# Gated recurrence: VectorE in place of GpSimd multiplies the matrix for the inverse by the step sizes, just ahead of turning it

## The reference, cut to what matters

```
def step(carry, inp):
    S, R = carry
    q_t, k_t, v_t, a_t, aR_t, b_t, g_t = inp
    kn = k_t / jnp.maximum(jnp.linalg.norm(k_t, axis=-1, keepdims=True), 1e-12)
    pred = jnp.einsum('bhji,bhj->bhi', S, kn)
    r = jnp.clip(v_t - pred, -CLIP, CLIP)
    S = a_t[..., None] * S
    kp = jnp.einsum('bhd,bhde->bhe', kn, S)
    S = S + b_t[..., None, None] * kn[..., None] * (v_t - kp)[..., None, :]
    o = jnp.einsum('bhji,bhj->bhi', S, q_t)
    R = aR_t[..., None] * R
    kpR = jnp.einsum('bhd,bhde->bhe', kn, R)
    R = R + g_t[..., None, None] * kn[..., None] * (r - kpR)[..., None, :]
    o = o + jnp.einsum('bhji,bhj->bhi', R, q_t)
    return ((S, R), o)
```

## Time and profile before

| | us |
|---|---|
| median of 3 runs | 2985.55 (2983.88 to 2993.01) |
| the profiled execution, its own time | 2989.19 |
| its span in the trace | 2987.4 |
| this sublayer's steady part in the trace (13 turns, 1052 to 1839) | 787 |

### The profile page before, as it was taken

The page is one execution under the profiler, slowest core; times in us unless marked ns, Lnnn a source line. Parts: engine busy times, 40 slices in busy tenths (PEclk is TensorE's granted clock), DMA queues, the critical chain, the costliest instruction groups (busy, mean ns, idle before and its releaser), DMA issues. The chain is left out here.

```text
span 2987.4 us, 115613 instructions
## 1 busy us (share of the span) xinstructions
PE 2398.5 (80%) x49947; PEld 1861.7 (62%) x49947; DVE 1954.5 (65%) x4625; ACT 1363.1 (46%) x3250; POOL 1002.2 (34%) x1250
## 2 busy tenths in 40 slices
PE   8987478999976578888778887669998997797754
PEld 6754465555555577777777776548776654575633
DVE  3448335777756787888777888157777666564752
ACT  5443133444443344454444542447776553563420
POOL 0000324556650345434543355311111440360004
PEclk9979677999997799999999999969999998897876
DMA  3200331111110000000000000012221003242014
GB/s 99 66 1 29 114 116 53 47 47 46 47 58 3 3 4 4 4 4 4 4 4 4 4 4 4 3 27 61 63 62 58 4 3 108 64 110 66 5 43 122
DMA packets 80270, 117.47 MB, mean 39 GB/s; under 512 B 11490, under 2 KB 66034, under 8 KB 79234
## 3 DMA queue, kind: packets, MB, share of 16 engines
q1 hardware_dynamic: 71250, 100.31, 10.9%
q0 software_dynamic: 8576, 10.53, 1.7%
HBM read 98.16 MB, written 16.51 MB: 38 GB/s over the span
## 5 line engine op out<-in xcount | busy, mean ns | idle before, releaser
L2469 POOL TENSOR_SCALAR l1xs_p<-l1xs_p,l1xs_col 128x257 f32<-128x257 f32 x256 | 234.3, 936 | 204.4 <-DVE l1xs_col L2425 204.4
L3173 PE MATMUL psum<-l1d_rw,l1d_cols 64*32 64x48 f32 x16384 | 188.1, 211 | 106.1 <-issue 76.1
L3173 PEld LDWEIGHTS psum<-l1d_rw,l1d_cols 64*32 64x32 f32 x16384 | 164.4, 108 | 128.5 <-issue 118.1
L2390 ACT ACTIVATE l1xs_p<-psum,l1xs_col 128x257 f32<-128x257 f32 x256 | 119.7, 473 | 209.6 <-DVE l1xs_col L2420 203.5
L3429 DVE TENSOR_TENSOR l1d_rw<-l1d_rw,l1d_tots 128x1536 f32<-128x1536 f32 (+1 forms) x96 | 141.4, 1473 | 64.9 <-PE psum L3173 64.3
L2945 POOL TENSOR_TENSOR l1d_kc<-l1d_ms,l1d_beta 128x512 f32<-128x512 f32 x16 | 17.5, 1093 | 494.9 <-DVE l1d_ms L3484 477.9
L2432 DVE STREAM_TRANSPOSE l1xs_pt<-l1xs_p 128x288 f32<-128x288 f32 x256 | 122.4, 478 | 79.1 <-POOL l1xs_p L2469 79.0
L3112 PE MATMUL psum<-XN,l1d_wp 128*128 128x128 f32 x1024 | 142.6, 296 | 7.6 <-issue 6.7
L3112 PEld LDWEIGHTS psum<-XN,l1d_wp 128*128 128x128 f32 x1024 | 130.6, 206 | 21.0 <-issue 17.8
L2354 PE MATMUL psum<-l1xs_pt,l1xs_vals 32*128 32x512 f32 x1152 | 136.6, 604 | 0.0
L2342 PE MATMUL psum<-l1xs_keys,l1xs_qx 128*32 128x257 f32 x2048 | 132.7, 392 | 3.7 <-DVE l1xs_qx L2414 1.9
(11 more groups left out here) (563 smaller groups left out, 6852.7 us busy)
## 6 DMA issues: line engine op xcount, KB each, us to landing
l2f_w<-in_l2f_w SPq DMA_DIRECT2D x16, 768.0 KB
l1xs_vals<-in_ctx_strips SPq DMA_DIRECT2D x16, 576.0 KB
l0f_w<-in_l0f_w SPq DMA_DIRECT2D x15, 579.0 KB
l0x_ctxT<-in_ctxT SPq DMA_DIRECT2D x16, 516.0 KB, 3.7
l1xs_keys<-in_ctxT SPq DMA_DIRECT2D x16, 516.0 KB
l2x_ctxK<-in_ctxT SPq DMA_DIRECT2D x64, 129.0 KB, 2.1
l2x_ctxV<-in_ctxT SPq DMA_DIRECT2D x64, 129.0 KB, 2.1
l3f_w<-in_l3f_w SPq DMA_DIRECT2D x15, 193.5 KB
```

Source lines behind the costliest of these rows:

```text
L2390: nc.scalar.activation(p[:, t % 4, :S2], score_ps(t)[:, :S2], ACT.Exp, bias=col[:, 0, t % 4:t % 4 + 1], accum_out=col[:, 1, t % 4:t % 4 + ...
L2469: nc.gpsimd.tensor_scalar(p[:, t % 4, :S2], p[:, t % 4, :S2], col[:, 2, t % 4:t % 4 + 1], None, ALU.mult).then_inc(s["norm"], 1)
L3173: mm = nc.tensor.matmul(k.ps[bank0 + pr + e // per * 2][b * T:b * T + T, e % per * w:(e % per + 1) * w], columns[rr, at:at + T], moving[rr ...
```

## The change

The two multiplications of `gather` leave POOL's list and go into DVE's, directly ahead of the transposes of `turn`. The wait for `mS` of the next tile at level 1 is dropped; the other waits stay. Tiles, shapes and arithmetic stay the same.

```diff
-            def gather(i):
-
-                pool.wait_ge(s["mS"], i * LEVELS + LEVELS)
-                pool.wait_ge(s["mR"], i * LEVELS + LEVELS)
-                pool.wait_ge(s["beta"], i + 1)
-                if i + 1 < NT:
-                    pool.wait_ge(s["mS"], (i + 1) * LEVELS + 2)
-                if i > 0:
-                    pool.wait_ge(s["wideX"], i * 2)
-                at = kc[:].rearrange("p (t c) -> p c t", t=T)
-                minus = beta[:, i % 3, 1].unsqueeze(2).to_broadcast([128, 2 * H, T])
-                tt(at[:, :H, :], ms[:, i % 2, :, 0, :], minus[:, :H], ALU.mult)
-                tt(at[:, H:, :], mr[:, i % 2, :, 1, :], minus[:, H:], ALU.mult).then_inc(s["kc"], 1)
-
...
             for i in range(NT):
-                gather(i)
                 pool.wait_ge(s["turn"], 2 * i + 2)
                 merge(i, 2)
...
+            def gather(i):
+
+                dve.wait_ge(s["mS"], i * LEVELS + LEVELS)
+                dve.wait_ge(s["mR"], i * LEVELS + LEVELS)
+                dve.wait_ge(s["beta"], i + 1)
+                if i > 0:
+                    dve.wait_ge(s["wideX"], i * 2)
+                at = kc[:].rearrange("p (t c) -> p c t", t=T)
+                minus = beta[:, i % 3, 1].unsqueeze(2).to_broadcast([128, 2 * H, T])
+                tt(at[:, :H, :], ms[:, i % 2, :, 0, :], minus[:, :H], ALU.mult)
+                tt(at[:, H:, :], mr[:, i % 2, :, 1, :], minus[:, H:], ALU.mult).then_inc(s["kc"], 1)
+
...
                 if i == NT:
+                    gather(i - 1)
                     turn(i - 1)
...
                 if mid and now:
+                    gather(i - 1)
                     turn(i - 1)
```

## The result

| | before | changed |
|---|---|---|
| median of 20 runs each, us | 2981.32 (2969.47 to 2993.01) | 2994.48 (2982.60 to 3000.67) |
| ratio, 95% interval | | 1.0039 (1.0027 to 1.0050) |
| profiled execution, us | 2989.19 | 2994.31 |
| its span in the trace, us | 2987.4 | 2992.4 |

The account below looks back on a forecast made before the run. A ring through DVE, POOL and PE bounds each tile; the later turn passes 14 us, PE's issue gaps return half, leaving 7 us: 2985.6 + 7 = 2992.5, rounded to 2992 us (+0.2%), range 2980 to 3005.

Parts of the forecast that it names:

- What bounds the kernel: Steady tile, 60.5 us: a ring through DVE, POOL and PE, where a late turn is late again at the turn back.
- The price of the pair: Two added DVE multiplications ahead of each turn: 1.15 us each, 2.2 us together, for the 128-byte write step.
- Rival B: The pair costs a plain 1.3 us; +2.5 us, 2988 us; chance 0.22.
- The relief: DVE at L3431 and L3429 no longer meets POOL's multiplication: 0.97 us gained in 5 of thirteen tiles.
- What passes of the delay: Turn's delay passes whole in six steady tiles, 9.2 us, and 4.7 us in eight others: together 14 us.
- The covers: DVE's waits for the broadcast at L3382 hide delay in eight steady tiles, 1.3 us a tile, unevenly spread.
- I take half, between all and nothing, because the rows give no finer measure: 14 / 2 = 7 us: PE's issue gaps shrink when PE waits and give back half of the 14 us delay, leaving 7 us.
- rival A with its covers: Issue gaps give nothing back, L3382 waits still hide part of the delay: 14 us, 2999.5 us; rival A's chance 0.28.
- the prediction's own sign of it: Rival A shows if PE's wait L3161 on L3373 grows from 6.1 us and its issue gaps stay.
- The last tile: DVE's gather meets the same wait for ACT's widening; 2.08 us of POOL become 2.2 us of DVE: nothing.

Follow-up runs that it names:

- the pair behind the turn: Kernel before, POOL's gather kept, plus the same two products written by DVE into an unread spare tile directly behind the turn: 1.0065, +19.4 us.
- the second trace: Another profile of the unedited changed kernel, taken with the experiments; thirteen periods from turn 1 to turn 14 take 796.9 us.
- the pair ahead of the turn: Kernel before, POOL's gather kept, plus the same two products written by DVE into an unread spare tile ahead of the turn: 1.0073, +21.7 us.
- the kernel before with two buffers: Kernel before with a second `kc` buffer, POOL keeping the gather: 0.9971, -8.7 us.
- the one with two buffers: Changed kernel with a second `kc` buffer, so the gather needs the widening of two tiles ago: 0.9998 of before.
- the pair in the wait: Kernel before, POOL's gather kept, plus two idle DVE products into a spare tile at the iteration's start, before the wait for `fill_0`: 0.9988, -3.6 us.
- POOL's gather beside the copies: Kernel before with two `kc` buffers, POOL's gather released by the next tile's `row0` instead of `mS` at level 1: 0.9990 of before.
- The pair twice: Changed kernel plus two idle DVE products into a spare tile between gather and turn in 15 tiles: 1.0105 of before, 19.7 us above changed.

## Why the prediction was right in kind and short in size

**What bounds the kernel: right.** That the place of DVE's work decides is shown by runs: one pair costs 21.7 us ahead of the turn, nothing in the wait for `fill_0`, and moving the gather from the one place to the other won 10 us back. That it is POOL's stretch which hands the delay on is read from the traces: the turn back waits for POOL in 13 of 13 tiles of the changed kernel. No run separates this from a simpler rival, by which it costs the same in any place of DVE's list that is not a wait; the pair behind the turn cost 19.4 us, and there it also made POOL's inverse longer. From turn to turn back no steady tile of any kernel took less than 23.5 us.

**The price of the pair: right.** 1.15 us each and 2.2 us together were forecast, 1.11, 1.05 and about 2.07 us measured. The reason is shown too: the step in what is written, alone, makes 0.70 us into 1.08 (mean of the two). The Trainium skill, page "SBUF — State Buffer", section "Door 1: The DMA port swizzle", says that consecutive accesses to one 16-byte line run at full bandwidth and each crossing to a new line pays; by that rule the trace agrees, for a write as well, at a factor of 1.5. Rival B, 1.3 us for the pair, falls.

**The relief: the mechanism was right, its size in the time is open.** L3431 on 448 numbers came down to 623 ns as forecast (630). I put the relief at 0.97 us in 5 tiles, 4.9 us. In the groups it is (781 - 623) x 26 = 4.1 us at that line and (1415 - 1228) x 26 = 4.9 us at its neighbour, of which I had counted 0.6 us; the second trace has the same means, 621 and 1229 ns. In the time two measurements disagree. It is 10.7 us, with some 8 us to either side, between the pair ahead of the turn and the changed kernel. But moving POOL's gather ahead of L3429 took away the same collision at the same place and came out 5.7 us slower, again with some 8 us to either side, as other instructions stretched and DVE's waits grew. My 4.9 us lies between the two.

**What passes of the delay: 14 us raw was near.** The covers were read at `keys` (L3382) alone. The trace after shows a second one that I missed, the 9.2 us for ACT ahead of the norms, which is gone; but the norms take 9.5 us longer in exchange (1730 for 999 ns, thirteen times), so little of it was a cover. In the second trace 5.9 us of that wait are left, and the norms take 4.6 us longer; in the kernel before with two buffers it is 5.4 us, so much of the difference is scatter. Both engines' lists agree with a partial cover: DVE's waits other than the turn back fell from 125.2 to 91.4 us (108.5 in the second trace), while PE's wait for the norms rose by 10.5 us (5.0).

**The step that failed is "I take half, between all and nothing, because the rows give no finer measure: 14 / 2 = 7 us".** PE's issue gaps gave back 1 us of 99.6, not 7, and grew where the delay was doubled. One trace alone would not carry this, since the gaps scatter. Counted from turn 1 to turn 14, they are 99.6 and 103.6 us in the two kernels without the change, with one buffer and with two, and 98.5, 100.5 and 99.4 us in the two traces of the changed kernel and the one with two buffers; but 89.5 us with the pair in the wait and 106.7 us with POOL's gather beside the copies. So a few microseconds may come back, and 7 is not seen.

The time of the pair ahead of the turn says it more strongly. By the prediction's own terms, without any relief, some 18 or 19 us of its delay should have passed the covers and half of that, 9 us, reached the end (an estimate, the 14 us and the relief of 4.9 us put back); measured are 21.7 us, 15.5 at least. The row that I drew on, 1.8 us of gaps beside an 11.6 us wait, came from one tile at the start. Why the steady part differs is not shown. Without the halving the sum is 2985.6 + 14 = 2999.6 us, +0.47%; measured is +0.39% (0.27 to 0.50), and the halved +0.23% lies outside. That is rival A with its covers, to which I gave a chance of 0.28, and the prediction's own sign of it was met: the wait L3161 on L3373 grew from 6.1 to 16.6 us and the gaps stayed. The pair twice cost 0.63 for each microsecond and the single one 0.7, which suggests that a cover of about a third stays in force and isn't used up by 2 us a tile; the intervals are too wide to show it.

**The last tile: nothing, right.** The gather waited 15.42 us for ACT on DVE as it had on POOL, and the last two turns are no further apart (44.0 us, before 46.7).

**What stays open.** What the relief of some 9 us in DVE's groups is worth in the time, for which the runs give 10.7 us one way and nothing the other. Whether the delay passes through POOL alone or through any place that is not a wait. And the clock's part: over the changed kernel's steady part the granted clock is 0.95 in one profiled execution and 0.92 in another, whose thirteen periods are 5.6 us longer, so part of the scatter may come with the clock; whether a later ring lowers it was not separated.

## What to carry to other kernels

Before work is moved between engines, ask what starts next from it: ahead of an instruction that starts another engine's rigid stretch it cost most of its length here (0.7 us for each us), directly behind it about as much, and in a wait of its own engine nothing, so the place in the list can matter more than the engine. Don't count on idle gaps elsewhere to give a delay back unless a row of the same stretch shows them shrink. Where an instruction is moved earlier, look at what the engine that it releases will then run beside: here the turn back's wait of 8 us in thirteen tiles went, and 78 us came in its place.

## What the runs showed of the hardware

- A VectorE multiplication of two SBUF tiles of 512 numbers a partition takes 0.72 and 0.68 us written in runs and 1.11 and 1.05 us written with a step of 128 bytes.
- VectorE instructions with two SBUF inputs stretch beside GpSimd's elementwise work on SBUF: 448 numbers from 0.62 to 1.47 us, 512 numbers from 0.69 to 2.00 us on average over twelve tiles, 480 from 0.65 to 1.65. The Trainium skill, page "SBUF — State Buffer", section "Who interferes with whom", says that a VectorE instruction with two SBUF inputs contends with a GpSimd instruction that reads SBUF; by that rule the trace agrees, and both lose (GpSimd's 1.09 us became 2.07).
- The small TENSOR_SCALAR of the norms (64 x 128 numbers) takes 0.22 us where GpSimd is idle (tile 1 of before) and 1.75 us where it starts beside GpSimd's `scale`.
